# Self-attention softmax: row maxima turned into rows by one product, copied by ScalarE, and added by one-hot weights in four row strips

## What is computed

```python
def _L0_attn_ref(x, Wqkv, bqkv, Wout, bout):
    qkv = (x @ Wqkv + bqkv).reshape(B, L, 3, H, Hd)
    ...
    q, k = apply_rope(q, k)
    scores = jnp.einsum('bhqd,bhkd->bhqk', q, k) / math.sqrt(Hd)
    probs = jax.nn.softmax(scores, axis=-1)
    out = jnp.einsum('bhqk,bhkd->bhqd', probs, v)
    ...
x = x + _L0_attn_ref(_layernorm(x, axis=-1), ...)
x = x + _L0_xattn_ref(_layernorm(x, axis=-1), ctx_1024, ...)
x = x + _L0_ffn_ref(_layernorm(x, axis=-1), ...)
x = x + _L1_attn_ref(_layernorm(x, axis=-1), ...)
x = x + _L1_xattn_ref(_layernorm(x, axis=-1), ctx_1024, ctx_1024, mask_SxS2_bk0, ...)
x = x + _L1_ffn_ref(_layernorm(x, axis=-1), ...)
```

## Time and profile before

| | |
|---|---|
| median of 3 runs | 1351.38 us (1351.25 to 1352.72) |
| the profiled execution's own time | 1354.58 us |
| its span in the trace | 1352.7 us |
| mean granted TensorE clock | 0.985 |
| busy: TensorE products, weight loads, VectorE, ScalarE, GpSimd | 95%, 85%, 73%, 62%, 35% |

### The profile page before, as it was taken

How to read it: one execution, slowest core, us unless ns; L and a number is a source line. 1 busy time by engine, 2 the same in 40 slices (tenths; PEclk the granted TensorE clock), 3 DMA queues, 4 the chain that set the end, 5 groups by cost and what they waited for, 6 DMA issues and landing times. The chain is left out here.

```text
span 1352.7 us, 40285 instructions
## 1 busy us (share of the span) xinstructions
PE 1278.7 (95%) x14932; PEld 1153.3 (85%) x14932; DVE 986.2 (73%) x2421; ACT 832.0 (62%) x1659; POOL 468.1 (35%) x576
## 2 busy tenths in 40 slices
PE   6999999899989999998999999999999998699997
PEld 5888888699979999998898888888777877589987
DVE  7888888456655555564888888887877788568886
ACT  4877777455655454553777777666666676356563
POOL 2232232122222122111000000056655567378884
PEclk9999999999988999999999999999999999899999
DMA  6000000031110000001010000000000000000000
GB/s 239 2 3 0 0 1 2 10 116 39 32 32 1 1 0 0 1 1 56 2 65 0 0 0 3 10 18 17 18 16 16 16 9 3 16 9 31 23 30 35
DMA packets 16884, 29.55 MB, mean 22 GB/s; under 512 B 3744, under 2 KB 7840, under 8 KB 16384
## 3 DMA queue, kind: packets, MB, share of 16 engines
q1 hardware_dynamic: 16768, 27.98, 6.3%
HBM read 23.78 MB, written 4.19 MB: 21 GB/s over the span
## 5 line engine op out<-in xcount | busy, mean ns | idle before, releaser
L853 ACT ACTIVATE a_probs<-a_S 128x512 f32<-128x512 f32 x384 | 205.7, 602 | 86.3 <-PE a_S L1314 46.2
L177 POOL TENSOR_TENSOR all_var_eps<-all_moments,all_ln_eps 128x2 f32<-128x2 f32 x96 | 24.3, 253 | 568.3 <-DVE all_moments L172 556.5
L1055 DVE TENSOR_REDUCE a_row_max<-a_S 128x4 bf16<-128x512 f32 x256 | 164.1, 682 | 16.7 <-PE a_S L1252 16.6
L806 POOL TENSOR_TENSOR a_shifts<-a_add_mask,a_cross_max 128x512 bf16<-128x512 bf16 x128 | 141.7, 1133 | 56.8 <-DVE a_cross_max L1055 56.8
L1326 PE MATMUL a_AV<-a_probs,a_v_pad 128*32 128x128 f32 x3072 | 103.8, 276 | 10.1 <-DVE all_odd_split L1068 6.2
L858 ACT ACTIVATE a_av_raw<-a_AV 128x512 f32<-128x512 f32 x96 | 57.5, 599 | 73.0 <-PE a_AV L1326 73.0
L1261 PE MATMUL a_S<-a_qm_hi,all_odd_split 32*128 32x256 f32 x1536 | 94.2, 301 | 6.0 <-DVE a_row_max L1055 2.2
L1326 PEld LDWEIGHTS a_AV<-a_probs,a_v_pad 128*32 128x32 f32 x3072 | 78.1, 109 | 24.8 <-issue 9.8
L105 PE MATMUL c_OUT<-all_odd_split,c_h_hi 128*128 128x256 f32 x512 | 94.6, 283 | 0.9 <-DVE all_x_res L1995 0.9
L1261 PEld LDWEIGHTS a_S<-a_qm_hi,all_odd_split 32*128 32x128 f32 x1536 | 68.9, 183 | 27.1 <-issue 11.6
L1055 DVE TENSOR_REDUCE a_cross_max<-a_S 128x4 f32<-128x512 f32 x128 | 82.6, 682 | 12.1 <-PE a_S L1284 12.1
(11 more groups left out here) (303 smaller groups left out, 4001.5 us busy)
## 6 DMA issues: line engine op xcount, KB each, us to landing
all_cx<-in_ctx_turned SPq DMA_DIRECT2D x16, 256.0 KB, 2.7
all_cx<-in_ctx SPq DMA_DIRECT2D x16, 256.0 KB, 2.7
out_x<-all_x_res SPq DMA_DIRECT2D x16, 256.0 KB, 2.0
all_x_res<-in_x SPq DMA_DIRECT2D x7, 512.0 KB, 7.4
b_routed_wi<-in_L_ffn_wi_W SPq DMA_DIRECT2D x1, 1024.0 KB, 5.2
b_routed_wo<-in_L_ffn_wo_W SPq DMA_DIRECT2D x1, 1024.0 KB, 8.0
all_even_weights<-in_L_ffn_W_fc SPq DMA_DIRECT2D x1, 1024.0 KB, 4.9
all_even_weights<-in_L_ffn_W_proj SPq DMA_DIRECT2D x1, 1024.0 KB, 6.9
```

Source lines behind the costliest of these rows:

```text
L806: pool.tensor_tensor(shifts[:, j], add_mask[:], cross_max[:, j, :].rearrange("p (h o) -> p h o", o=1).to_broadcast([P, QH, P]), ALU.subtra ...
L853: act.activation(probs[:, b * NQ + j, :], S2[j][:], ACT.Exp, scale=DH ** -0.5).then_inc(exp_ok, 1)
L1055: dve.tensor_reduce((cross_max if at(G)[0].cross else row_max)[:, j, :], S1[j][:].rearrange("p (h k) -> p h k", h=QH), AXX, ALU.max).then_ ...
```

## The change

A new product `turn_maxima` makes one bf16 product of `row_max` with the identity: the maxima of all 16 heads come out as rows in bank `S1[3]`, heads of bank j at partitions 32j to 32j + 3 (so `row_max` gets 32 columns a bank, 28 of them zero). ScalarE copies these 128 x 128 values to `max_rows` (`take_rows`). `shift_scores` then uses products of 32 rows: the stationary operand is a column of `minus_rows_b` that holds -1 at row h of each strip, broadcast to 128 columns, and the moving operand is the strip of `max_rows`. The order is head by head and within a head strip by strip, so four products in a row go to four strips and four banks. `shift_scores` waits for the copy and releases all four banks by its last four products. `transposes(G + 2)` now stands ahead of the shift for all layers. The matrix `minus_rows` comes by a transfer of its own; a product that folds the value bias (once, in a1) is moved behind the shift.

```diff
-        self.from_dram = {k: a[k] for k in ("ident", "head_mask", "turn_sign")}
+        self.from_dram = {k: a[k] for k in ("ident", "head_mask", "turn_sign", "minus_rows")}
...
-        dve.tensor_scalar(tiles["neg_ident_b"][:], tiles["ident"][:], -1.0, None, ALU.mult).then_inc(self.ready, 1)
+        dve.tensor_copy(tiles["minus_rows_b"][:], tiles["minus_rows"][:]).then_inc(self.ready, 1)
...
-    row_max = sb("row_max", [P, 4, QH], BF16)
+    row_max = sb("row_max", [P, 4, 32], BF16)
+    max_rows = sb("max_rows", [P, P], BF16)
...
+            pool.memset(row_max[:], 0.0).then_inc(rows_zero, 1)
...
+            def take_rows(G, b):
+
+                act.wait_ge(rows_full, G * PAIR + b + 1)
+                at_least(act, s2_full, step(G, b, 0))
+                act.activation(max_rows[:], S1[NQ - 1][:, 0:P], ACT.Copy).then_inc(rows_ok, 1)
...
+                if inside(G) and not at(G)[0].cross:
+                    take_rows(G, 0)
                 for j in range(NQ):
                     if inside(G):
                         exp_step(G, 0, j)
...
                 piece(G, 4)
+                if inside(G) and not at(G)[0].cross:
+                    take_rows(G, 1)
                 if rope and inside(G + 1) and not at_first(G, -1):
                     masked_k(G + 1, odd, 1)
...
+            def turn_maxima(G, b):
+
+                pe.wait_ge(max_ok, step(G, b, NQ))
+                pe.matmul(S1[NQ - 1][:, 0:P], row_max[:].rearrange("p j h -> p (j h)"), ident_b[:], start=True, stop=True,
+                          skip_group_check=True).then_inc(rows_full, 1)
+
             def shift_scores(G, b):
...
+                if not at(G)[0].cross:
+                    pe.wait_ge(rows_ok, G * PAIR + b + 1)
+                    for h in range(QH):
+                        for j in range(NQ):
+                            strip = slice(32 * j, 32 * j + 32)
+                            last = pe.matmul(S2[j][:, h * P:(h + 1) * P], minus_rows_b[strip, h:h + 1].to_broadcast([32, P]),
+                                             max_rows[strip, :], start=False, stop=h == QH - 1, skip_group_check=True)
+                            if h == QH - 1:
+                                last.then_inc(s2_full, 1)
+                    return
...
                 if inside(G):
                     scores(G, 0, parity)
+                    if not at(G)[0].cross:
+                        turn_maxima(G, 0)
                 if inside(G - 1):
                     turn((G - 1) * PAIR + 1)
                 piece(G, 0)
-                if late and normed_here(G + 2):
+                if normed_here(G + 2):
                     transposes(G + 2)
                 if inside(G):
                     shift_scores(G, 0)
-                if not late and normed_here(G + 2):
-                    transposes(G + 2)
```

More of the change, by code:

```diff
@@ L622, in attention_stage @@
     sb, sem = nm.sb, nm.sem
-    ident, ident_b, neg_ident_b, head_mask = (consts[k] for k in ("ident", "ident_b", "neg_ident_b", "head_mask"))
+    ident, ident_b, minus_rows_b, head_mask = (consts[k] for k in ("ident", "ident_b", "minus_rows_b", "head_mask"))
     N = NG * len(layers)
@@ L682, in attention_stage @@
     x_first, x_second, x_rest, mask_in = (sem(n) if (n == "mask_in") == cross else None for n in ("x_first", "x_second", "x_rest", "mask_in"))
+    rows_zero, rows_full, rows_ok = sem("rows_zero"), sem("rows_full"), sem("rows_ok")
     zeroed, setup, setup_pe = sem("zeroed"), sem("setup"), sem("setup_pe")
@@ L1054, in max_step @@
                 at_least(dve, s2_full, T - 3)
-                dve.tensor_reduce((cross_max if at(G)[0].cross else row_max)[:, j, :], S1[j][:].rearrange("p (h k) -> p h k", h=QH),
+                if is_first(G) and b == 0 and j == 0:
+                    dve.wait_ge(rows_zero, 1)
+                dve.tensor_reduce((cross_max if at(G)[0].cross else row_max)[:, j, 0:QH], S1[j][:].rearrange("p (h k) -> p h k", h=QH),
                                   AXX, ALU.max).then_inc(max_ok, 1)
@@ L1298, in scores @@
                         s2_pass(b, j, par, i // 3, i % 3)
+            def turn_maxima(G, b):
+                pe.wait_ge(max_ok, step(G, b, NQ))
+                pe.matmul(S1[NQ - 1][:, 0:P], row_max[:].rearrange("p j h -> p (j h)"), ident_b[:], start=True, stop=True,
+                          skip_group_check=True).then_inc(rows_full, 1)
             def shift_scores(G, b):
-                made, n = at(G)[0].cross, at(G)[1]
+                if not at(G)[0].cross:
[8 more added lines that the diff above has]
+                    return
+                n = at(G)[1]
                 for j in range(NQ):
-                    if made:
-                        pe.wait_ge(shift_ok, step(n, b, j) + 1)
-                    else:
-                        pe.wait_ge(max_ok, step(G, b, j) + 1)
+                    pe.wait_ge(shift_ok, step(n, b, j) + 1)
                     for h in range(QH):
-                        part = S2[j][:, h * P:(h + 1) * P]
-                        if made:
-                            last = pe.matmul(part, shifts[:, j, h, :], ident_b[:], start=False, stop=h == QH - 1,
-                                             skip_group_check=True)
-                        else:
-                            last = pe.matmul(part, row_max[:, j, h:h + 1].to_broadcast([P, P]), neg_ident_b[:],
-                                             start=False, stop=h == QH - 1, skip_group_check=True)
+                        last = pe.matmul(S2[j][:, h * P:(h + 1) * P], shifts[:, j, h, :], ident_b[:], start=False, stop=h == QH - 1,
+                                         skip_group_check=True)
                     last.then_inc(s2_full, 1)
@@ L1439, in first_half @@
                 odd = 1 - parity
-                late = inside(G) and at(G)[0].cross
                 if inside(G):
                     scores(G, 0, parity)
+                    if not at(G)[0].cross:
+                        turn_maxima(G, 0)
                 if inside(G - 1):
@@ L1473, in second_half @@
                     scores(G, 1, parity)
+                    if not at(G)[0].cross:
+                        turn_maxima(G, 1)
                     turn(G * PAIR)
-                if second is not None and at_first(G, NG - 2):
-                    pe.wait_ge(max_ok, step(G, 1, NQ))
-                    second.wt.wait_split(pe)
-                    value_bias(S1[NQ - 1])
                 piece(G, 4)
@@ L1484, in second_half @@
                     shift_scores(G, 1)
+                if second is not None and at_first(G, NG - 2):
+                    second.wt.wait_split(pe)
+                    value_bias(S1[NQ - 1])
                 if not late and turned_context:
@@ L2392, in layout @@
         "ident": np.eye(P, dtype=np.float32),
+        "minus_rows": -(p[:, None] % 32 == np.arange(QH)[None, :]).astype(np.float32),
         "head_mask": ((p[:, None] // DH) % HV == np.arange(HV)[None, :]).astype(np.float32),
```

4 lines of the change are left out of this document (2 added, 2 removed).

## The result

The changed kernel takes 1361.82 us, the median of 7 runs (1359.84 to 1367.99). The kernel before takes 1351.38 us over 7 runs (1351.09 to 1354.48). The ratio is 1.0078, with a 95% interval of 1.0062 to 1.0093: **slower by 0.8%, 10.4 us**. The forecast was 1365 us, slower; the time is inside its range of 1356 to 1376.

The account below looks back on a forecast made before the run. The prediction took each half to be set by when maximum_scores may start: TensorE's queue or the third exponential. Terms 4.7 + 7.5 + 1.0 + 0.35 - 1.1 + 1.4 + 0.45 = 14 us gave 1365 us, range 1356 to 1376.

Parts of the forecast that it names:

- 0.13 us of cover: First half, kernel before: the time the exponentials have to spare before maximum_scores would wait for the third one, 0.13 us.
- TensorE's terms: Shift on TensorE's queue: product, two switches and strips take 0.70 us against 0.94, winning 0.24 us a half.
- The product: turn_maxima on TensorE's queue: one more bf16 product, put at 0.06 us.
- The switch into strips: TensorE going from full-array products to 32-row strips ahead of the shift: put at 0.2 us.
- The strips with the switch out: The shift's 16 strip products, 0.24 us, plus the return to full-array products, 0.2 us.
- The rival with a nearly free switch: Switch into strips nearly free: first halves lose 0.19 and 0.27 us instead of 0.39 and 0.47; 1360 us, chance 0.10.
- the one with 0.11 a step: Rival: strips go at the loads' pace, 0.11 us a step, first exponential another 0.15 later; 1374 us, chance 0.16.
- First halves: Self-attention's first halves: first exponential 0.65 us later, maximum_scores 0.39 later, or 0.47 in the hardware loops.
- Second halves: No transposes ahead of the shift: maximum_scores at 3.80 after scores, -0.07 us a half written out, +0.09 in the loops.
- two releases: Looped second halves: the copy and the exponential each start later after a release, together +0.16 us.
- the start: Ahead of the first scores: one more constant transfer puts VectorE's first work and all behind it back by 0.45 us.
- The rival with the other sign: TensorE's queue decides, so the 0.24 us a half is saved in 62 halves, 15 us; 1337 us, chance 0.07.

Follow-up runs that it names:

- e2: The kernel before with its old shift, only transposes(G + 2) moved ahead of the shift, no strips and no copy; 1359.17 us, ratio 1.0053.
- e8: The changed kernel with eight unused bf16 products ahead of maximum_scores in every first half of self-attention; 1363.99 us, ratio 1.0085.
- e9: The changed kernel with eight unused bf16 products ahead of maximum_scores in every second half of self-attention; 1372.68 us, ratio 1.0143.
- e5: e1 without strips: one-hot stationary operands over all 128 rows, bank by bank, each bank released after its four products; 1369.57 us, ratio 1.0115.
- e4: The kernel before with turn_maxima and ScalarE's copy added, their rows unused, and the old shift kept; 1357.44 us, ratio 1.0035.
- e3: The changed kernel with the strips' 16 products written bank by bank, four in a row to the same strip; 1363.09 us, ratio 1.0083.
- e1: The changed kernel with the shift again ahead of the transposes in first halves of self-attention; 1351.12 us, ratio 0.9993.
- e7: e1 with the old shift in the first half of each layer's group 0 only; 1351.83 us, ratio 0.9994.
- e6: e1 with the old shift in six halves where copy or fourth maximum lacks cover, value bias at its old place; 1351.30 us, ratio 0.9982.

## Why the prediction was right, and which terms were off

**What bounds the kernel** was read rightly: `maximum_scores` may start after the third exponential or when TensorE gets there, and 0.13 us of cover is thin. e2 shows it with the old shift, e8 for first halves, and e9 shows how near the two are in second halves.

**TensorE's terms.** Forecast: 0.24 won per half; measured 0.33.
- The product was put at 0.06 and costs the queue 0.01 (206.71 to 206.72): `turn`'s loads go on under it.
- The switch into strips was 0.2 and is: from the transposes' first load to the strips' it is 0.64, where e2 takes 0.44 to the first load of the old shift. I had put the transposes at 0.39; right behind `turn` they take 0.05 more, in e2 as well.
- The strips with the switch out were 0.24 + 0.2 and take 208.09 - 207.75 = 0.34. How it divides the runs don't tell.

Together 0.24 + 0.05 - 0.05 + 0.10 = 0.34, near the 0.33 read off. The rival with a nearly free switch falls with the 0.64, the one with 0.11 a step with a span of 0.23 for all sixteen loads.

The weights of 16 products in strips and a switch take 0.34 where the full array takes 0.85 (e5), 2.5 times less. By the Trainium skill, TensorE: Matmul & The Clock Gate, Measured speedup vs the span model, four row strips give 3.07 times, measured there with 512 columns. The trace, with 128, has 3.9 times for the loads alone (0.23 against e5's 0.90), less than the page's figure with the switch out (2.5), and 1.6 with both switches counted (0.54).

**First halves.** The mechanism held: shift behind the transposes, one release, exponentials late, `maximum_scores` idle. The first exponential came at 2.39 instead of 2.48. The strips began at 1.96 as forecast (1.95), their last load at 2.10 instead of 2.13 (207.75 + 0.23 - 0.09), and from there to ScalarE it took 0.29 instead of 0.35. The half lost 0.27 instead of 0.39; over 28 halves 9.3 us instead of 12.2. The copy took 0.277 us for a forecast 0.28 and ended at 1.51, hidden.

**Second halves** were the weakest step: "the third ends 2 x 0.49 + 0.60 later at 3.73, `maximum_scores` at 3.80". The exponentials started at 1.97 and not 2.15: the strips loaded at 1.52 instead of 1.62, their last at 1.66 instead of 1.80, and ScalarE followed after 0.31 instead of 0.35. The third ended at 3.53. But `maximum_scores` loaded 0.22 after it, at 3.76, where I had 0.07. Two waits of TensorE's sequencer lie in these 0.22 (217.06 and 217.17 in the trace); what else does, the runs don't tell. These two errors nearly cancelled in the written-out halves. In the loops they didn't. I had charged 0.16 us for two releases, which is about right: the first exponential came at 2.10, 0.13 later than in the written-out halves. But the start from 2.15 was wrong there as well, and in layer 0 `maximum_scores` follows the third exponential (3.68) after 0.05 to 0.06, at 3.74. In layer 1 it loads at 3.78, behind `output`; that wait was forecast ("it would let `maximum_scores` load at about 3.8 too"):

```profile
767.49 0.19 PEld L1276 LDWEIGHTS a_S<-a_qm_hi,all_odd_split 32*128 32x128 f32 x4 [0.20 <-DVE a_row_max L1070]
...
771.27 0.30 PEld L1267 LDWEIGHTS a_S<-a_km,a_q_hi 32*128 32x128 f32 x8
```

The loops' second halves won 2.1 us where I had them lose 1.4.

**Left out of the sum**: the late fourth maximum, the half with the value bias, and the slower clock in group 0's second half (below), together 5 us in the profiled execution. Left open: the start. The trace of after has `scores` 0.44 later, as forecast, but e4, which has no additional transfer, starts at 27.72 against 26.61 in before, and e3, which has it, at 26.73. One trace of each does not tell this term from chance.

**The rival with the other sign** needed the first exponential at most 0.13 us later. e1 comes nearest (0.17 later) and still gives no more than no change: the strips' saving on TensorE is real, but first halves can't use it, since the detour by product, copy, switch and single release costs the exponentials what the queue wins.

## What to carry to other kernels

Before making an engine's queue shorter, find who would be waited for next and measure the slack there: here 0.13 us of cover decided about 0.33 us of saved work a half. A step that feeds another engine should stand ahead of work that feeds nobody soon, and one release for four consumers makes the first of them as late as the last; strips that run side by side give just that, whatever order the code writes (e3). Keep a new stage away from places where its input is late or nothing hides it: six such halves of 64 cost 2.4 us in e1, more than that kernel won in all.

## What the runs showed that I had not expected

- **The order written inside the strips doesn't matter** for sixteen 128-column bf16 products: written four in a row to one strip (e3) the loads span 0.26 us, written strip by strip 0.23. In both the four products that come last in their strips are the last four to start.
- **Stretches of TensorE's clock at its lower level.** In after the records show short stretches at 1.2 instead of 2.4 GHz inside this attention, at 39, 664 and 879 us among others; the half from 34.47 to 42.99 has a mean of 0.80 and takes 1.67 us longer than its counterpart, which stayed at 1.00 (both shown under e7). The half ahead doesn't tell the cases apart. From 27.05 on TensorE was busy for 6.64 of 7.41 us (first row), in before for 6.76 of 6.79 (second), but in e9 for 6.70 of 7.46 (third), and e9 has no stretch there.

```profile
27.05:34.46 7.41, 6.64 (x109) 5.54 (x109) 6.41 (x13) 4.44 (x9) 1.09 (x1) 1.00 0.01 3
26.61:33.40 6.79, 6.76 (x108) 6.07 (x109) 6.32 (x13) 4.33 (x8) 1.09 (x1) 1.00 0.01 4
27.72:35.18 7.46, 6.70 (x109) 5.59 (x110) 6.46 (x13) 4.44 (x9) 1.09 (x1) 1.00 0.01 3
```

  What goes with the stretch is the idle time just ahead of it. Group 0's second half has no `output`, so a quicker shift leaves TensorE's loads idle for longer ahead of `maximum_scores`, 2.00 us in after (first) for 1.34 in before (second):

```profile
38.22 0.33 PEld L1267 LDWEIGHTS a_S<-a_km,a_q_hi 32*128 32x128 f32 x8 [2.00 <-issue]
37.03 0.33 PEld L1252 LDWEIGHTS a_S<-a_km,a_q_hi 32*128 32x128 f32 x8 [1.34 <-issue]
```

  After, e1, e3, e6, e7 and e8 have 1.97 to 2.01 us there in both layers, and eleven of these twelve halves have the stretch (e7's in layer 1 has not); it begins between 0.1 us ahead of that load and 1.6 behind it. Before, e2, e4, e5 and e9 have 1.30 to 1.45, and none of their ten halves has it; e5 has one a half earlier, at 30. e9 is after with eight more products in this idle time. So the stretch comes with the longer idle time, and not with the first half's wait for the copy (e7). That the idle time alone makes the clock fall isn't shown: e7's layer 1 had it without.
- **Most of the spread between runs goes with the clock**: 0.83 us for each 0.001 of mean granted clock. e6's twelve runs, 10.5 us apart, lie within 1.1 us (standard deviation) of one line. Versions less than 0.3% apart should be compared over a dozen runs, and at equal clock only where neither brings slow stretches of its own.
